# A chunked selective scan: running sums of the decays from one matmul and from transfers, in place of one chain of matmuls for every chunk

## The reference

```
dA = minimum(exp(dt * A), 0.99)              # one decay for each token and head
h  = clip(dA_t * h + outer(x_t, B_t), -10, 10)
y_t = C_t . h
```

## Time and profile before

| | us |
|---|---|
| median of 3 runs (lowest to highest) | 1808.78 (1807.62 to 1810.61) |
| the profiled execution, its own time | 1805.59 |
| its span, first to last instruction | 1803.7 |
| PE busy | 1699.5 (94%) |
| DVE busy | 1589.2 (88%) |
| ACT busy | 1475.9 (82%) |
| POOL busy | 645.7 (36%) |

### The profile page before, as it was taken

The page is one execution under the profiler, slowest core; times in us unless marked ns, Lnnn a source line. Parts: engine busy times, 40 slices in busy tenths (PEclk is TensorE's granted clock), DMA queues, the critical chain, the costliest instruction groups (busy, mean ns, idle before and its releaser), DMA issues.

```text
span 1803.7 us, 40081 instructions
## 1 busy us (share of the span) xinstructions
PE 1699.5 (94%) x15395; PEld 663.1 (37%) x15396; DVE 1589.2 (88%) x2294; ACT 1475.9 (82%) x2806; POOL 645.7 (36%) x932
## 2 busy tenths in 40 slices
PE   6899999999999999999999999999999879899884
PEld 4432222222222222278722222222222345366553
DVE  7999999999999999945499999999998477588678
ACT  5679999999999999943389999999999757777555
POOL 1432310222444444100035566555610133133447
PEclk9999999999999999999999999999999989999897
DMA  4522222111221122178511211222102243422121
GB/s 127 175 71 85 89 68 65 57 59 35 74 58 54 59 62 68 55 212 228 161 47 52 68 49 44 54 60 60 41 12 57 67 122 113 143 72 66 50 64 47
DMA packets 152765, 142.15 MB, mean 79 GB/s; under 512 B 40394, under 2 KB 131533, under 8 KB 152418
## 3 DMA queue, kind: packets, MB, share of 16 engines
q1 hardware_dynamic: 144226, 122.37, 23.5%
q0 software_dynamic: 8352, 17.29, 3.3%
HBM read 76.60 MB, written 60.03 MB: 76 GB/s over the span
## 4 chain that ended last, share of the span: by engine, by line
PE 82%; ACT 9%; DVE 6%; issue 2%; DMA 1%; POOL 1%; SPq 0%; DVEq 0%; ACTq 0%
PE PS L2037 30%; PE PS L2136 18%; PE PS L2021 11%; ACT probs L1350 7%; PE PS L2086 4%; PE PS L2071 2%; PE PS L2341 2%; PE PS L2323 2%; PE PS L2180 1%; PE PS L2186 1%; PE PS L2259 1%; PE PS L2344 1%; PE PS L2063 1%; PE PS L2407 1%; PE PS L2326 1%
## 5 line engine op out<-in xcount | busy, mean ns | idle before, releaser
L908 DVE TENSOR_REDUCE mxp<-PS 128x1 f32<-128x1024 f32 x1024 | 1170.7, 1213 | 22.0 <-PE PS L2021 17.2
L1350 ACT ACTIVATE probs<-PS 128x512 f32<-128x512 f32 x2048 | 1096.3, 597 | 68.2 <-PE PS L2136 24.0
L2037 PE MATMUL PS<-probs,VH 128*32 128x256 f32 x8192 | 643.0, 391 | 2.2 <-ACT probs L1350 1.0
L2136 PE MATMUL PS<-stacks 51*128 51x512 bf16 x2048 | 442.2, 388 | 21.3 <-ACT probs L1350 17.6
L2021 PE MATMUL PS<-stacks 48*128 48x512 bf16 x2048 | 416.2, 380 | 2.8 <-DVE mxp L908 1.7
L2037 PEld LDWEIGHTS PS<-probs,VH 128*32 128x32 f32 x8192 | 172.9, 108 | 399.5 <-issue 220.3
L2136 PEld LDWEIGHTS PS<-stacks 51*128 51x128 bf16 x2048 | 115.8, 93 | 461.1 <-ACT probs L1350 380.1
L1716 POOL DMA_INDIRECT S<-oe_d,ROWI x128 | 130.0, 1015 | 133.8 <-PE PS L2037 126.1
L1686 POOL DMA_INDIRECT xe_d<-S,ROWI x128 | 125.3, 979 | 139.1 <-PE PS L2037 115.7
L1664 POOL CAST spl<-nmx 128x8 bf16<-128x8 f32 x64 | 12.7, 199 | 304.7 <-DVE nmx L864 226.6
L2021 PEld LDWEIGHTS PS<-stacks 48*128 48x128 bf16 x2048 | 105.2, 95 | 21.3 <-DVE mxp L908 6.8
(11 more groups left out here) (363 smaller groups left out, 1816.2 us busy)
## 6 DMA issues: line engine op xcount, KB each, us to landing
stacks<-qkl_d SPq DMA_DIRECT2D x128, 96.0 KB
xe_d<-zt SPq DMA_DIRECT2D x16, 640.0 KB
XNT<-xe_d SPq DMA_DIRECT2D x32, 320.0 KB, 3.8
oe_d<-XNT SPq DMA_DIRECT2D x32, 320.0 KB, 3.2
stacks<-qkl_d SPq DMA_DIRECT2D x128, 64.0 KB
o_d<-SG SPq DMA_DIRECT2D x256, 32.0 KB
ews<-in_ew_dram SPq DMA_DIRECT2D x33, 192.0 KB, 2.4
stacks<-qkl_d SPq DMA_DIRECT2D x128, 32.0 KB
```

The source lines that it names most:

```text
L908: v.tensor_reduce(mxp[:, n // 2, n % 2:n % 2 + 1], MXB[n % 2].rearrange("p a c -> p (a c)"), X_AX, ALU.max).then_inc(mx_done, 1)
L1350: act.activation(probs[:, at:at + 512], PS[:, bank_of(u, e), :], ACT.Exp, scale=float(1.0 / np.sqrt(np.float32(DK)))).then_inc(exp_done, 1)
L2037: mm = pe.matmul(OB[32 * jg:32 * jg + 32, c:c + 256], VH[w][:, kt, :], probs[:, at:at + 256], start=(kt < 2 and half == 0), stop=(kt >= TC ...
L2136: pe.matmul(PS[:, bank_of(u, e), :], KS[w][o:o + KROWS + 3, kt * P:(kt + 1) * P], QS[w][o:o + KROWS + 3, q0:q0 + 512], start=True, stop=Tr ...
```

## The change

The log decays `DT` (128 tokens of a tile on partitions, 32 tiles x 4 heads on columns) are summed once, by two f32 matmuls of 128 columns (`decay_sums`): once with tile and head on partitions and tokens on columns (copied to `LR`, stored to DRAM as `rows_d`), once the other way round (negated into `NL`). For each chunk SP then loads the rows back with `load_decays(c)`: L(t) of the 8 pairs on all 128 partitions (512 KB, into one of three buffers `LW`), and L(t) by batch entry on 64 partitions each (2 x 128 KB, into `LE`). VectorE's `decay_args(c)` makes `min(L(t) - L(s), mask)` in place by eight instructions with a column of `NL` as the scalar operand; the mask is 0 or -10000. ScalarE's exponential then gives the masked matrix `DM` at once and `DMb` from the same buffer. `chunk_sums`, `spread_decays` and the mask's multiplication are gone. `el_done` is set one exponential earlier.

```diff
+            def load_decays(c):
+                w = c % 3
+                hold(opb_ready, c - 2)
+                rows = rows_d.rearrange("(b c) n -> c b n", b=B)[c]
+                sp.dma_start(LW[w]..., rows.unsqueeze(0).broadcast_to([P, B, NH1 * P])).then_inc(lw_ld[w], 16)
+                for b in range(B):
+                    sp.dma_start(LE[w][rows_of(b), :], rows[b:b + 1, :].broadcast_to([DS, NH1 * P])).then_inc(le_ld[w], 16)
...
-                    load_chunk(0)
+                    load_b_c(0)
+                    hold(rows_out, ROWS_OUT + 1)
+                    sp.dma_start(rows_d.rearrange("t (h s) -> (t h) s", h=NH1), LR[:, :]).then_inc(rows_st, 16)
+                    load_b_x(0)
+                    hold(rows_st, ROWS_ST + 16)
+                    load_decays(0)
                     load_chunk(1)
+                    load_decays(1)
+                    load_decays(2)
...
+            v.tensor_scalar(d0, d0, -1.0, float(np.log(0.99)), ALU.mult, ALU.min).then_inc(dt_set, 1)
+            v.wait_ge(sums_ready, 1)
+            v.tensor_copy(LR[:, :], PS[:, 7, 0:P]).then_inc(rows_out, 1)
+            v.wait_ge(sums_ready, 2)
+            link(v.tensor_scalar(NL[:, :], PS[:, 1, 0:P], -1.0, None, ALU.mult))
...
-            def spread_decays(c):
-                after(v, la_ready, c)
-                link(v.tensor_copy(ldc[:, :, :].unsqueeze(2), ldt[:, :, c:c + 1, :]))
-                v.tensor_tensor(lb, TRI..., ldc..., ALU.mult).then_inc(lb_set, 1)
+            def decay_args(c):
+                w = c % 3
+                v.wait_ge(lw_ld[w], LW_BASE + 16 * (c // 3 + 1))
+                for b in range(B):
+                    for h in range(NH1):
+                        i, col = b * NH1 + h, (b * TCH + c) * NH1 + h
+                        ins = v.scalar_tensor_tensor(LW[w][:, i, :], LW[w][:, i, :], NL[:, col:col + 1], PAST, ALU.add, ALU.min)
+                ins.then_inc(args_set, 1)
...
-                v.tensor_tensor(DM, DE, TRI..., ALU.mult).then_inc(dm_done, 1)
...
-                act.wait_ge(la_ready, c + 1)
+                act.wait_ge(args_set, c + 1)
                 after(act, ops_ready, c)
-                act.activation(DE, PS[:, 0:2, :]..., ACT.Exp).then_inc(d_done, 1)
+                act.activation(DM, LW[c % 3], ACT.Exp).then_inc(d_done, 1)
...
+            def decay_sums():
+                pe.wait_ge(dt_set, 1)
+                decays = DT.rearrange("p t h -> p (t h)")
+                pe.matmul(PS[:, 7, 0:P], decays, TRI, start=True, stop=True).then_inc(sums_ready, 1)
+                pe.matmul(PS[:, 1, 0:P], TRI, decays, start=True, stop=True).then_inc(sums_ready, 1)
...
-            def chunk_sums(c):
-                pe.wait_ge(lb_set, c + 1)
-                after(pe, d_done, c)
-                scaled = lb.rearrange("p (b h) t -> p b (h t)", b=B)
-                for b in range(B):
-                    pe.matmul(PS[:, b, :], BELOW, scaled[:, b, :], start=True, stop=True)
-                after(pe, el_done, c)
-                for b in range(B):
-                    mm = pe.matmul(PS[rows_of(b), 7, :], onesq[:, 0:DS], scaled[:, b, :], start=True, stop=True)
-                mm.then_inc(la_ready, 1)
```

More of the change, by code:

```diff
@@ L151, in build @@
         lda_d = dram("lda_d", (N, NH1))
+        rows_d = dram("rows_d", (NT, NH1 * P))
         y_d = dram("y_d", (N, DI))
@@ L249, in build @@
         sc_aff = sb("sc_aff", [P, 3, DI])
-        lb, DE, DM, MM0 = (VP[:, 8 * i:8 * i + 8, :] for i in range(4))
+        LW0, LW1, DM, MM0 = (VP[:, 8 * i:8 * i + 8, :] for i in range(4))
+        LW = [LW0, LW1, waq[:, 4:6, :, :].rearrange("p i t c -> p (i t) c")]
         MM = [MM0, YM[:, 0:8, :]]
@@ L353, in build @@
         tile_ld = [sem(f"tile_ld{i}") for i in range(4)]
[L354 to L355 removed]
+        dt_set, sums_ready, args_set, gg_set, d_done, el_done, opb_ready, vr_out, ops_ready, c_done, y_out, hs_done = (
+            sem(n) for n in ("dt_set", "sums_ready", "args_set", "gg_set", "d_done", "el_done", "opb_ready", "vr_out", "ops_ready", "c_done", "y_out", "hs_done"))
+        lw_ld, LW_BASE = m_ld[0:3], 64 * UNITS // 4
+        le_ld, LE_BASE = qk_ld[1:4], 192 * UNITS // 4 + 32
+        rows_out, ROWS_OUT = h_carried, 1
+        rows_st, ROWS_ST = xct_st, 16
         bnd_read, yc_ready = sem("bnd_read"), sem("yc_ready")
@@ L637, in _, with load_b_c @@
                     expert_io()
+            def load_decays(c):
+                w = c % 3
+                hold(opb_ready, c - 2)
+                rows = rows_d.rearrange("(b c) n -> c b n", b=B)[c]
+                sp.dma_start(LW[w].rearrange("p (b h) t -> p b (h t)", b=B), rows.unsqueeze(0).broadcast_to([P, B, NH1 * P])).then_inc(lw_ld[w], 16)
+                for b in range(B):
+                    sp.dma_start(LE[w][rows_of(b), :], rows[b:b + 1, :].broadcast_to([DS, NH1 * P])).then_inc(le_ld[w], 16)
             def load_chunk(c):
+                load_b_c(c)
+                load_b_x(c)
+            def load_b_c(c):
                 w = c % 4
@@ L701, in _ @@
             hold(bct_st, 32 * NB)
-            for c in range(2, TCH):
+            for c in range(2, 4):
                 load_chunk(c)
+            for c in range(3, TCH):
+                load_decays(c)
+                if c >= 4:
+                    load_chunk(c)
             xg = xs_d.rearrange("(t p) c -> p t c", p=P)
@@ L1100, in chunk_operands @@
                 if c + 1 < TCH:
-                    spread_decays(c + 1)
+                    decay_args(c + 1)
                 v.wait_ge(d_done, c + 1)
-                v.tensor_tensor(DM, DE, TRI.unsqueeze(1).broadcast_to([P, B * NH1, P]), ALU.mult).then_inc(dm_done, 1)
                 v.wait_ge(tile_ld[c % 4], TILE_BASE + 96 * (c // 4 + 1))
@@ L1139, in _ @@
             router_scores()
+            decay_args(0)
             chunk_operands(0)
@@ L2363, in router_rows @@
                 pe.matmul(PS[:, 2, 304:304 + B], ones1[:, :], s1_[:, 1, :], start=True, stop=True).then_inc(l1_ready, 1)
-            chunk_sums(0)
             router_logits()
@@ L2370, in _ @@
             for c in range(TCH):
-                if c + 1 < TCH:
-                    chunk_sums(c + 1)
                 chunk_products(c)
@@ L2494, in layout @@
         "ident": np.eye(P, dtype=f),
-        "consts": np.concatenate([level, end, tri, np.repeat(np.eye(B), DS, axis=0), 1 - tri], axis=1).astype(f),
+        "consts": np.concatenate([level, end, tri, np.repeat(np.eye(B), DS, axis=0), -1e4 * (1 - tri)], axis=1).astype(f),
         "hz": states.astype(f),
```

33 lines of the change are left out of this document (16 added, 17 removed).

## The result

| | kernel before | changed kernel |
|---|---|---|
| time of 4 runs each, median | 1809.26 us (1807.62 to 1810.61) | 1844.91 us (1842.48 to 1845.43) |
| profiled execution | 1805.59 us, span 1803.7 | 1845.43 us, span 1843.6 |
| mean granted clock of TensorE | 0.981 | 0.934 |

The changed kernel is about 2% slower: ratio 1.0207, 95% interval 1.0195 to 1.022. The forecast was 1849.0 in a range of 1822 to 1860. The ratios in this document leave out two executions that lie over 1.5% above the fastest of their kernel: 1847.30 us (24 at the head, 4 a chunk) and 1916.80 us (rows of chunk 3 earlier).

The account below looks back on a forecast made before the run. TensorE was taken to bound the scan, busy 119.96 of 122 us. Loop +31.9, last chunk +1.3 and head +7.1 sum to 40.3 on the profiled 1805.6, giving 1845.9; 3.2 more for the median gives 1849, range 1822 to 1860.

Parts of the forecast that it names:

- Clock at 0.50 from first to last chunk: TensorE in the scan: without chunk_sums its clock stays at 1.2 GHz in every chunk; chance 0.80.
- The two waits in each chunk: TensorE's waits in the scan loop, one of about 1 us and one of 0.4 us, named beside the low clock.
- The low ring: Scan loop, TensorE and VectorE waiting on each other at the low clock: 10.2 us a chunk.
- The scale of 1.84: TensorE's small products in the scan: at the low clock they take 1.84 times their full-clock time, 3.56 against 1.93 us.
- +31.9: Scan loop: 15 chunks at the low clock take 153.0 us against 121.06, +31.9 us (+23 to +38).
- the ring's two bounds: Scan loop at the low clock: 9.6 us if L2339 and L2316 were not slowed, 10.6 with all at 2 times.
- The full-clock ring, 6.86: Scan loop, TensorE and VectorE waiting on each other at full clock: 0.94 + 4.03 + 1.89 = 6.86 us a chunk.
- Rival F: TensorE's clock in the scan stays full or returns in the first chunks: loop -18.2, total -11, 1798 us; chance 0.11.
- VectorE's eight: VectorE in each chunk: eight 128-column instructions with a per-partition scalar take 2.16 us, between 1.2 and 2.7.
- The head, +7.1: Start of the scan: chunk 0 waits behind chunk 1's rows, its CTD ending at 1583.2 instead of 1576.08, +7.1 us (+5 to +11).
- Over 6 us of slack: Row loads in the steady scan loop: over 6 us between landing and L1135, so they were costed at nothing.
- Last chunk +1.3: End of the scan: the last chunk runs low from its start rather than from 1699.6, +1.3 us.

Follow-up runs that it names:

- 24 at the head, 4 a chunk: Changed kernel plus unread 512-column matmuls on TensorE, 24 once ahead of the first products and 4 behind each chunk's; 1805.97 us, ratio 1.0022 to the kernel before.
- rows of chunk 3 earlier: Changed kernel with reordered loads, 28 unread wide matmuls ahead and six a chunk, plus chunk 3's rows issued in SP's wait for the last stores; 1798.51 us.
- six fillers: Changed kernel plus six unread bf16 matmuls of 512 columns on 128 partitions behind each chunk's products; ten runs 1803.00 us, ratio 0.9966 to the kernel before.
- one-partition fillers: Changed kernel plus six unread bf16 matmuls of 512 columns, each on one partition, behind each chunk's products; 1872.48 us, ratio 1.0346 to the kernel before.
- sums on constants: Changed kernel plus the four former f32 matmuls of chunk_sums at each chunk's head, on constant data with the result unread; 1814.39 us in one run.

## Why the prediction was right, step by step

- **Clock at 0.50 from first to last chunk: right**, and shown by the experiments to be the cause. It is worth 10.03 - 6.79 = 3.24 us a chunk, taken with six fillers in the 6.79. The two waits in each chunk that the prediction named beside it are not needed: without any gap the clock stayed low too. The argument from the earlier trace rows, that the same small products ran at 0.50 for five busy us without bringing it back, was the one that carried; here they did so for 154 us. The Trainium skill (TensorE: Matmul & The Clock Gate, What's actually happening) says that activity releases the reduced clock, by time and not by the number of matmuls. These traces disagree as far as "activity" is read as a busy TensorE: 80 of 80 us busy stayed at 1.2 GHz, and with six wide matmuls a chunk, in a loop busy for 77.30 of 80 us, it ran at 2.4.
- **The low ring, 10.2 us: right in its mechanism, and its sum in part by luck.** In steady state it is 10.03, 0.17 less than reckoned. Its terms by the rows above: L2374 3.61 (reckoned 3.56), L2377 to L2360 1.77 (1.8), L2360 to L1151 0.77 (0.87), L2372 1.05 (1.13). The scale of 1.84 in place of 2 was about right. Over 15 steps the 0.17 would make the loop 2.6 us shorter than forecast; two long steps that the prediction did not have, 11.54 and 11.42 us, add 2.9. So the +32.1 against +31.9 is closer than the terms deserve. Added up again, the ring's two bounds are 9.3 and 10.7, not 9.6 and 10.6; 10.03 lies inside either pair.
- **The full-clock ring, 6.86: right**, 6.79 with the fillers in. Rival F's price for the loop was thus sound; only its condition did not come about. No run shows it without extra matmuls. The kernel with six fillers, whose clock was low in its first chunks, ended 6 us below the kernel before, where the rival had 11.
- **VectorE's eight: right**, 2.19 us against 2.16, the case of the earlier trace rows.
- **The head, +7.1: a little short**, +7.9. The mis-sized term is the landing of chunk 1's rows: 6.4 us after their issue (1572.74 to 1579.10), where I took 4.7 between the bounds 2.9 and 8.8. Chunk 0's rows took 6.55 us (1567.34 to 1573.89). I had chosen the wrong side of the middle: with SP's other loads in flight (235 GB/s in that stretch) the broadcast's 512 KB stood nearer to twice the 4.4 of the earlier trace rows than to the bare 2.9. SP's issue of those rows was 1.1 us earlier than reckoned, of which 0.6 is `DT` being ready earlier, and that made up for part of it.
- **"Over 6 us of slack" for the rows: wrong once.** In steady state no wait for rows shows up. But chunk 3's rows were late by 4.68 us, since SP issued the loads of chunks 2 and 3 first. It cost 11.54 - 10.03 = 1.5 us. The other long step, 11.42, has no wait for rows.
- **Last chunk +1.3: right**, +1.25. What I did not have is the 1.3 that the stages behind gained.
- The parts come to 7.9 + 32.1 + 1.25 - 1.3 = 39.9, against a sum of 40.3. The medians' difference is 35.7: the median of before was 3.7 above its profiled run, that of the changed kernel 0.5 below its own. My step of adding the 3.2 us of before to the changed kernel put the forecast 4 us too high.

## What to carry to other kernels

Before taking wide matmuls out of a loop that is left with small ones, look in the trace for a stretch in which the small ones run alone, and read whether the granted clock rises in it: that the engine is busy does not answer this. Where the clock stays low, a few unread wide matmuls in the engine's own wait can be worth more than the change itself: here they turned +2.1% into -0.3 to -0.6%. And a load that is moved earlier on one queue is only won if the loads that it passes have slack of their own.

## What the runs showed of the chip that I had not expected

- A TensorE that is busy for 80.00 of 80 us, on matmuls of one partition or of 64 f32 columns, stays at a granted clock of 0.50; it did so to the end of the scan. Between the one-partition fillers and the wide ones only the number of partitions differs, so in this loop it made the difference. The first fall of the clock in the kernel before fits this: it came behind 3.70 us without a gap on 512-column matmuls of 32 partitions. Whether it was the width or the type that made the 64-column ones fail was not tried.
- With the sums on constants, the clock fell to 0.50 for some 3 us in the middle of a stretch from 1593 on in which TensorE was busy in every us.
- Adding 1.47 us of TensorE work to each chunk shortened it from 10.03 to 6.79 us.
- A broadcast of 512 KB to all partitions took 6.36 and 6.55 us from issue to use beside SP's other loads, while 256 KB in a plain load took 2.9.
